# Two of TensorE's written-out programs become loops on the engine: the ranks of the edges and the second half of layer 0

## The reference

```python
def gnn_layer(x, W, b, src, dst):
    h = x @ W.T + b
    msgs = h[src]
    agg = jax.ops.segment_sum(msgs, dst, num_segments=N_NODES)
    return jax.nn.relu(agg)

h = gnn_layer(x, W1, b1, src, dst)
out = gnn_layer(h, W2, b2, src, dst)
...
h = jnp.maximum(_layernorm(x, axis=-1), 0.0)
x = x + _L0_gnn_ref(h, edge_index, L0_gnn_W1, L0_gnn_b1, L0_gnn_W2, L0_gnn_b2)
```

## Time and profile before

| what | value |
|---|---|
| median of 3 runs | 2800.92 us (2797.36 to 2803.63) |
| the profiled execution, its own time | 2799.54 us |
| its span | 2797.8 us |
| PE busy | 2459.9 us, 88% |
| DVE busy | 2024.5 us, 72% |
| POOL busy | 1709.9 us, 61% |
| ACT busy | 1373.6 us, 49% |

### The profile page before, as it was taken

How to read it: one execution, slowest core, us unless ns; L and a number is a source line. 1 busy time by engine, 2 the same in 40 slices (tenths; PEclk the granted TensorE clock), 3 DMA queues, 4 the chain that set the end, 5 groups by cost and what they waited for, 6 DMA issues and landing times. The chain is left out here.

```text
span 2797.8 us, 46999 instructions
## 1 busy us (share of the span) xinstructions
PE 2459.9 (88%) x13660; PEld 2095.8 (75%) x13660; DVE 2024.5 (72%) x5281; ACT 1373.6 (49%) x2875; POOL 1709.9 (61%) x1832
## 2 busy tenths in 40 slices
PE   3555379998988886999999969999999699999998
PEld 3344268887877776999999958888888588888886
DVE  7777666664655554888877869999999666666666
ACT  1555334454776764555555523333333245555553
POOL 0565345554566765777777647777777445555553
PEclk9999999999999998999999989999999799999999
DMA  8677643533444543343333333333334245555553
GB/s 246 206 209 206 196 125 113 146 119 114 127 134 145 156 151 127 111 129 115 113 118 114 107 110 123 114 115 114 116 120 121 85 139 153 153 153 153 153 152 110
DMA packets 145287, 385.55 MB, mean 138 GB/s; under 512 B 34127, under 2 KB 34287, under 8 KB 144554
## 3 DMA queue, kind: packets, MB, share of 16 engines
q0 software_dynamic: 100144, 300.93, 36.0%
q1 hardware_dynamic: 45002, 83.04, 9.5%
HBM read 259.61 MB, written 148.26 MB: 146 GB/s over the span
## 5 line engine op out<-in xcount | busy, mean ns | idle before, releaser
L1830 ACT CAST d_Thi<-d_pt 128x512 fp32r<-128x512 f32 x79 | 46.4, 587 | 307.8 <-DVE d_pt L787 276.7
L1678 PE MATMUL c_pu<-c_Zhi,parts 128*128 128x256 f32 x640 | 182.0, 284 | 5.3 <-DVE c_Zlo L1596 5.3
L1680 PE MATMUL c_pu<-c_Zhi,parts 128*128 128x256 f32 x640 | 181.8, 284 | 0.0
L1679 PE MATMUL c_pu<-c_Zlo,parts 128*128 128x256 f32 x640 | 180.6, 282 | 0.0
L815 POOL DMA_INDIRECT f_Gsrc<-rows,indexS x79 | 76.0, 962 | 170.4 <-PE f_phsrc L2159 161.4
L2075 ACT ACTIVATE f_Mhi<-f_pm 128x512 fp32r<-128x512 f32 x79 | 47.3, 598 | 262.2 <-DVE f_pm L2108 255.6
L2099 DVE TENSOR_TENSOR f_Hlosrc<-f_phsrc,f_Hhisrc 128x512 fp32r<-128x512 f32 x79 | 54.6, 692 | 159.6 <-ACT f_Hhisrc L2069 127.7
L794 PE MATMUL b_po<-parts,b_Thi 128*128 128x512 f32 x316 | 132.4, 419 | 41.0 <-issue 26.1
L819 POOL DMA_INDIRECT h<-a_rows,indexD x79 | 79.6, 1008 | 117.7 <-ACT a_rows L1172 109.0
L1565 ACT ACTIVATE c_pu<-c_pu,c_b1col 128x256 f32<-128x256 f32 x160 | 61.6, 448 | 167.6 <-PE c_pu L1680 167.6
L794 PE MATMUL d_po<-parts,d_Hhi 128*128 128x512 f32 x316 | 131.2, 415 | 1.9 <-DVE d_Hlo L1848 1.9
(11 more groups left out here) (451 smaller groups left out, 9548.0 us busy)
## 6 DMA issues: line engine op xcount, KB each, us to landing
rows<-r_xt SPq DMA_DIRECT2D x40, 520.0 KB
h<-q_zerorow SPq DMA_DIRECT2D x80, 256.0 KB
r_xt<-in_x SPq DMA_DIRECT2D x80, 256.0 KB
a_wstage<-in_L_W SPq DMA_DIRECT2D x3, 1024.0 KB
selrowsD<-selD SPq DMA_DIRECT2D x1, 2640.0 KB
selrowsS<-selS SPq DMA_DIRECT2D x1, 2640.0 KB
q_keyrowD<-in_dst POOLq DMA_DIRECT2D x1, 2560.0 KB, 17.0
q_keyrowS<-in_src POOLq DMA_DIRECT2D x1, 2560.0 KB
```

Of the source, the lines that this page charges most:

```text
L1678: pe.matmul(psum_u[:, o, :], g.Whi[2][:, c, cols], Zhi[:, c, :], start=c == 0, stop=False)
L1679: pe.matmul(psum_u[:, o, :], g.Whi[2][:, c, cols], Zlo[:, c, :], start=False, stop=False)
L1680: ins = pe.matmul(psum_u[:, o, :], g.Wlo[2][:, c, cols], Zhi[:, c, :], start=False, stop=c == C - 1)
```

## The change

In the ranks the body is two tiles long where it was eight, and `pipeline` runs it over 40 groups: 4 tiles are written out, a loop of 36 passes of 2 tiles follows, and 3 tiles are written out at the end. In the second half of layer 0 `pipeline` takes the place of `straight` with the same body of four tiles: the groups up to 1 are written out, a loop of 16 passes of 4 tiles follows, and the last two groups are written out.

```diff
                 def body(i):
-                    for u in range(U):
-                        at(i, u, 0, U, ET, look)
-
-                straight(GR, 0, 0, body)
+                    for u in range(2):
+                        at(i, u, 0, 2, ET, look)
+
+                pipeline(pe, -(-ET // 2), 0, 0, body)
...
             if second:
-                straight(GR, 1, 0, body)
+                pipeline(pe, GR, 1, 0, body)
```

## The result

The changed kernel takes 2804.62 us (median of 19 runs), the kernel before 2799.41 us beside it (also 19). The two medians lie 5.2 us apart. One of the 19 executions of the changed kernel took 5047.27 us; it counts as a slow one and is not in the ratio. The result is inside the range, and within the 0.2% that I called no change, but it is not nothing: the interval excludes the forecast of +0.6 us. The direction of the small remainder was one that I had priced at +3 us and then set to zero.

A forecast was written before the change was run, and what follows sets the result against it. The prediction took POOL's rows of indirect DMA issues, which hold TensorE's signals, to bound both stages. It summed 2800.92 + 0.6 (ranks loop entry and exit) + 0 (layer 0's second half) = 2801.5 us, range 2780 to 2828.

The forecast's parts named there:

- the forecast of +0.6 us: Whole kernel: only the ranks loop's entry and exit cost time, 0.3 us each; 2801.5 us, chance 0.50.
- What bounds the stages: Ranks and layer 0's second half: POOL's rows of issues and held TensorE signals set the time, not TensorE's program reading.
- the neighbour's rows: Layer 0's first half: written-out tiles 3.88 us apart, looped 3.87, so a loop in the second half adds 0.
- The other marks: Profile after: about 85 us idle before L509, near 29 at L393, ranks 261 us within 3.
- The price of the steps: Ranks, between the table's arrival and L509: fused and register steps add 0.13 us, taken as 0.2 with handover.
- The step that failed: Ranks, waits for TensorE: signals are held until POOL's row ends, so 0.2 us more delay is absorbed; cost 0.
- three values that I had worked out for the ranks: Ranks: 0 if holds absorb the delay, +3 us if 16 waits pay 0.2 us, +24 if every tile pays 0.3.
- S: Rival, ranks: the L509, ACT copy, next L509 chain sets the pace; +16 to +24 us, 2817 to 2825; chance 0.22.
- F: Rival, both stages: holds belong to written-out programs and vanish with loops; 2760 or 2731 us; chance 0.08.
- P: Rival, both loops: each of 52 jumps back fetches an instruction page again; +45 us, 2846; chance 0.04.
- G: Rival, both stages: later TensorE breaks up POOL's rows of six, some holds fall away; 2781 to 2787 us; chance 0.12.
- the forecast's own upper edge: Whole kernel: some 0.03 of the forecast's 0.50 chance lies above 2806.5 us, where a result counts as slower.

The follow-up runs named there:

- e2_b_loop: Kernel before with only TensorE's second half of layer 0 turned into a loop, its ranks left written out: ratio 1.0003 (0.9993 to 1.0012).
- e12_steps1: Kernel before, ranks written out, with one empty semaphore step on TensorE between the table's arrival and the first L509: ratio 1.0012 (1.0003 to 1.0021).
- e8_f_rows: Kernel before with one extra POOL gather per tile in layer 3's tiles 20 to 39, two in tiles 40 to 59: 2840.14 us, one execution.

## Why the prediction was right, and where not

**What bounds the stages** held. TensorE's reading of its program is not a bound anywhere, and the second half of layer 0, where I had taken 0 by the neighbour's rows, is the same within what the ratio can tell (e2_b_loop), if perhaps 1 to 2 us longer by the traces. Its idle time in front of L794, 41.7 us, is what was forecast. The other marks that the prediction set for itself missed: it said about 85 us in front of L509 (99.8), near 29 at L393 (39.9), and the ranks within 3 us of before (3.7 more). Its reading of 16 waits at L393 left out three put down to "remote"; with them the 28.9 us are 19 waits.

**The price of the steps** was right. I had put the steps ahead of L509 at 0.2 us, and the trace of after has 0.21. The branches were taken as covered, and the loops of two, four and eight and the one step without a branch agree with it. They take 215 ns at the median there:

```profile
L73 PEldq ALU_OP  x36: 32/32/32, 80.6 to 310.7; - x36
L73 PEldq COMPARE_BRANCH  x36: 83/215/233, 80.7 to 310.8; - x36
```

**The step that failed** is "an L509 that is 0.2 us later only waits 0.2 us less to be let through. Then it is 0." The 2.07 us were read at the wrong signal, the one from TensorE's L509 to ACT. What VectorE waits for at that place is L516 of the tile ahead of that L509, and that signal came earlier, at 159.45, 0.31 us after POOL's row and ahead of the rest. For it the added delay is not absorbed: it misses its early moment and comes with the rest, 1.07 us after the row, so VectorE waits 2.24 us in place of 1.47. Nine picks made this step, so a delay of 0.1 or 0.2 us turned into some 0.75 us each. Why a signal comes at the one moment or the other is not known; that an empty step of 0.09 us is enough to change it in nearly every rhythm is what e12_steps1 shows. Of the three values that I had worked out for the ranks (0, +3, +24) the middle one is what came: +3.7 us in the trace, +3.9 us by the ratio. That it agrees is luck, since the working behind it (0.2 us at each of 16 waits) is in proportion to the delay, and the cost is not: 0.09 us costs about as much, and 2.4 us no more by the ratio.

**The rivals.** S, at every tile +0.2 to 0.3 us, would have been 2817 to 2825. VectorE waits at the pick of S in 19 of 79 tiles after the change, as before it, not in half of them. F fell with the first look at the trace of after, which has the holds still, and with e8_f_rows. P, a page fetched at each jump, is out: fewer pages were fetched, 36 against 52. The Trainium skill ("Runtime: NRT & Kernel Launch", section "Instruction fetch mechanics") says that instructions are fetched in blocks of 16 KiB and that a taken branch has to wait for a fetch where its target is outside the current window of two pages. 0.59 MB in 36 packets is 16 KB each, and the number of packets went down with 52 jumps back, so the trace agrees with the first and shows no fetch for a jump. G, the reverse of what came, did not happen: in the trace of after POOL's rows of six are still there, and the delay made the holds in front of VectorE longer.

**The chances.** I had 0.47 for no change beyond 0.2% and the result lies there; the 0.03 that I gave the forecast's own upper edge and the missing middle case between it and S should have been one case of its own, at +3 to +5 us, where the result fell between the forecast and S.

## What to carry to other kernels

Where engines wait for one another in a fixed rhythm and signals come through in bursts, ask of a small delay which signal it pushes over an edge, not how much it adds. And read the hold at the signal that the busiest engine waits for, not at a neighbour's. In such a place the price of an added step need not be in proportion to its length. Put an instruction behind a wait only if the engine that waits for the answer has slack there: of the loop's steps here, those that ran ahead of the wait (branches and counters, some 0.3 us a pass) cost nothing that could be measured, and 0.09 us behind it cost about 3 us. Turning TensorE's program into a loop was nearly free in the stage where its matmuls run back to back (3.88 and 3.87 us a tile).

## What the runs showed of the hardware

Signals of TensorE can reach their waiters microseconds late while POOL issues indirect DMAs one behind another, 0.3 us apart. In the ranks before, 79 of 168 with a record are over 0.5 us late, up to 3.1 us, and most late ones come through together about 1.0 to 1.4 us after the last issue of the row. With two gathers more per tile in layer 3 (e8_f_rows) it is up to 6.8 us. VectorE's signals are held too, but less: in the ranks before 30 of 420 with a record are over 0.5 us late, and none in the second half of layer 0, where 104 of 211 of TensorE's are. Of ACT's signals none with a record (156 in the ranks, 406 in the second half of layer 0, looked at where a semaphore is ACT's alone) is over 0.1 us late. Rows of six issues with at least 6 us between them (layer 1) held no signal of TensorE.

An empty semaphore increment on TensorE costs about 0.15 us where several follow each other (2.4 us for sixteen, 0.55 for four), three times the 50 ns of a fused register step, and a single one behind the wait adds 0.09 us. A compare-and-branch on TensorE's queue takes 215 ns at the median in the ranks' loop; the Trainium skill ("Advanced Engine Details and Errata", section "Control Flow Timing") gives about 108 ns, and here the measurement decides.
